# Copying node rows within memory during the sort, and making layer-1 node rows beside two attention hops

## What is computed

```python
# layer 0: attention over edges, then five propagation steps
s = leaky_relu(sum(tanh(x[src] @ W_h) * a_h) + sum(tanh(x[dst] @ W_t) * a_t) + s_rel[type])
A = 0.9 * segment_softmax(s, src)
Z = x for 4 heads
for _ in range(5):
    Z = segment_sum(A * Z[dst], src) + 0.1 * x
out = Z @ W_o
# x1 = x + out, then (out - mean) / sqrt(var + eps) over the 64 features   (a "layer-1 row")
# layer 1: four rounds of a graph convolution, layer 2: Chebyshev, layer 3: GIN with batch norm
```

## Time and profile before

| what | value |
|---|---|
| median of 3 runs | 10182.19 us (10180.14 to 10186.59) |
| profiled execution | 10185.65 us |
| its span | 10183.8 us |
| busy: PE, DVE, ACT, POOL | 57%, 66%, 30%, 70% |
| mean granted TensorE clock | 0.702 |
| HBM read, written | 852.84 MB, 795.02 MB |

### The profile page before, as it was taken

The page is one execution under the profiler, slowest core; times in us unless marked ns, Lnnn a source line. Parts: engine busy times, 40 slices in busy tenths (PEclk is TensorE's granted clock), DMA queues, the critical chain, the costliest instruction groups (busy, mean ns, idle before and its releaser), DMA issues. The chain is left out here.

```text
span 10183.8 us, 117523 instructions
## 1 busy us (share of the span) xinstructions
PE 5768.8 (57%) x28479; PEld 4109.1 (40%) x28479; DVE 6707.0 (66%) x13870; ACT 3105.4 (30%) x5997; POOL 7153.1 (70%) x7145
## 2 busy tenths in 40 slices
PE   3856999500000001886777786767774769833338
PEld 2453333100000001775666565555553658733336
DVE  8954333387878787996777786877775767622227
ACT  2542222163222222443434342222221432200006
POOL 2564777577777777777777676767776767677764
PEclk9978999755555555887877897777676775555559
DMA  0074333164545454437867676654444984311127
GB/s 14 7 244 125 73 72 74 36 212 156 167 145 166 147 166 135 128 121 187 222 214 227 208 259 203 229 166 142 136 135 132 332 271 131 106 46 47 45 63 278
DMA packets 1256873, 1519.22 MB, mean 149 GB/s; under 512 B 835537, under 2 KB 956719, under 8 KB 1256634
## 3 DMA queue, kind: packets, MB, share of 16 engines
q1 hardware_dynamic: 995656, 1253.98, 37.8%
q0 software_dynamic: 252192, 248.44, 11.0%
q10 hardware_dynamic: 8786, 14.21, 0.4%
HBM read 852.84 MB, written 795.02 MB: 162 GB/s over the span
## 5 line engine op out<-in xcount | busy, mean ns | idle before, releaser
L2764 POOL DMA_INDIRECT r_got<-state,comb_src x1176 | 1139.3, 969 | 367.6 <-issue 344.1
L336 POOL DMA_INDIRECT payload_or_bias_rows<-payload,place x784 | 779.1, 994 | 477.7 <-issue 252.2
L1949 PE MATMUL hop_ps_into<-hop_out,span_s 128*128 128x256 f32 x8 | 4.9, 715 | 1865.6 <-DVE hop_out L1759 1865.6
L1540 POOL DMA_INDIRECT hop_got<-edges_b,next_col x784 | 825.0, 1052 | 254.9 <-issue 237.5
L1540 POOL DMA_INDIRECT hop_got<-edges_a,next_col x784 | 782.6, 998 | 259.4 <-issue 238.5
L1949 PEld LDWEIGHTS hop_ps_into<-hop_out,span_s 128*128 128x128 f32 x8 | 2.0, 311 | 1866.2 <-DVE hop_out L1759 1866.2
L3043 PE MATMUL r_ps_v<-dense1g,r_gt 128*128 128x128 f32 x4312 | 752.8, 343 | 0.0
L3043 PEld LDWEIGHTS r_ps_v<-dense1g,r_gt 128*128 128x128 f32 x4312 | 681.2, 247 | 160.6 <-issue 160.6
L1838 ACT COPY hop_got<-hop_zeros 128x1792 f32<-128x1792 f32 x224 | 378.1, 1688 | 1091.3 <-DVE hop_ps_msg L1704 1082.0
L2924 DVE TENSOR_REDUCE r_stat<-r_sq 128x14 f32<-128x896 f32 x448 | 483.9, 1080 | 272.9 <-ACT r_sq L3097 271.5
L2869 DVE SCALAR_TENSOR_TENSOR r_acc<-r_acc,r_runs_now,r_got 128x64 f32<-128x64 f32 (+1 forms) x1564 | 447.9, 286 | 254.0 <-DMA r_got<-state,comb_src 197.9
(11 more groups left out here) (779 smaller groups left out, 17457.9 us busy)
## 6 DMA issues: line engine op xcount, KB each, us to landing
state<-r_y SPq DMA_DIRECT2D x252, 448.0 KB, 3.7
r_in<-state SPq DMA_DIRECT2D x252, 448.0 KB, 4.5
edges_a<-hop_out SPq DMA_DIRECT2D x112, 896.0 KB, 4.3
edges_b<-hop_out SPq DMA_DIRECT2D x112, 896.0 KB, 4.3
hop_side<-x_dst SPq DMA_DIRECT2D x280, 224.0 KB, 4.0
own<-plain_y SPq DMA_DIRECT2D x56, 952.0 KB
g_rows<-r_gx SPq DMA_DIRECT2D x112, 448.0 KB, 2.6
x_and_sums<-c_y SPq DMA_DIRECT2D x56, 896.0 KB
```

What stands on the lines that cost most here:

```text
L336: nc.gpsimd.indirect_dma_start(out=t.raw[:, n, :], out_offset=None, in_=t.pay[k], in_offset=bass.IndirectOffsetOnAxis(t.place[:, k, n:n + ...
L1540: pool.indirect_dma_start(out=got[:, u, c, :], out_offset=None, in_=table, in_offset=at, bounds_check=EP - 1, oob_is_err=False).then_inc(g ...
L2764: pool.indirect_dma_start(out=got[:, n, c - b * CT, :], out_offset=None, in_=table, in_offset=bass.IndirectOffsetOnAxis(idx[:, at + c:at + ...
```

## The change

- The sort's block: ScalarE, right after it stores the payload rows, issues 18 copies from `x` straight to `t.nodes1`, within memory: 8 for the second half of the wide rows (272 bytes a row, taken from `x` with the first numbers of the next row behind it), 2 for the last row of each partition, 8 for the first half (256 bytes a row). Nobody waits for them in this block. The clears go to SP, behind `store_keys`.
- `EARLY` is 250 and `UNDER_DEGREES` 272: 42 more payload gathers lie in the histogram, 22 (for 14) in the degrees' block, 120 (for 170) in the block behind it.
- `plain_rows` is gone. `store_marks` takes its place: 8 stores of 16 bytes for each node into the wide rows, four on SP and four on ScalarE; SP waits for them and for the copies.
- The target's part of a wide row is now gathered from its start, `[x, marks]`, 68 numbers and not 65.
- Hops 1 and 2 each make the layer-1 rows of half the nodes, 7 columns of 128 a turn, and SP stores them over the copied `x` in the first 64 numbers of the wide rows.

```diff
-EARLY = 208
-UNDER_DEGREES = 222
+EARLY = 250
+UNDER_DEGREES = 272
@@ sort_sources, ScalarE
-            act.wait_ge(blank_made, 1)
...
+            for n in range(X_PIECES):
+                lo_n, hi_n = n * J // X_PIECES, min((n + 1) * J // X_PIECES, J - 1)
+                with_next = bass.AP(x.tensor, x.offset + lo_n * D, [[J * D, P], [D, hi_n - lo_n], [1, ROW]])
+                act.dma_start(places[:, lo_n:hi_n, PLAIN:WIDE], with_next).then_inc(t.x_placed, 16)
...
+            for n in range(X_PIECES):
+                some = slice(n * J // X_PIECES, (n + 1) * J // X_PIECES)
+                act.dma_start(places[:, some, X1], given[:, some, :]).then_inc(t.x_placed, 16)
             act.wait_ge(pay_put, 16)
@@ store_marks (for plain_rows)
+        def pieces(eng, parity):
+            places = t.nodes1.rearrange("(p j) w -> p j w", p=P)
+            for n in range(parity, MARK_PIECES, 2):
+                some = slice(n * J // MARK_PIECES, (n + 1) * J // MARK_PIECES)
+                eng.dma_start(places[:, some, MARKS:MARKS + 4], t.marks[:, some, :]).then_inc(stored, 16)
@@ edge_pass of hops 1 and 2, SP: behind the side load of this turn, ahead of the result store of the last
+                        for i, u in ago(0):
+                            past(sp, xt_done, i, u, 2)
+                            sp.dma_start(xin[:, u % 2], w["x"]...[:, node_columns(i, u), :]).then_inc(xin_in[u], 16)
+                        for i, u in ago(3):
+                            sp.wait_ge(xy_ready[u], i + 1)
+                            sp.dma_start(t.nodes1...[:, node_columns(i, u), X1], xy[:, u]).then_inc(xy_kept[u], 16)
@@ VectorE: behind the linked sums of this turn
+                    for i, u in ago(2):
+                        dve.wait_ge(xroot_ready[u], i + 1)
+                        nc.vector.reciprocal(xstat[:, u % 2, 2, :], xstat[:, u % 2, 1, :]).then_inc(xinv_ready[u], 1)
+                    for i, u in ago(1):
+                        dve.wait_ge(xsq_ready[u], i + 1)
+                        nc.vector.tensor_reduce(xstat[:, u % 2, 0, :], xsq[:, u % 2], AX.X, ALU.add).then_inc(xsum_ready[u], 1)
@@ ScalarE: at the start of the turn
+                    for i, u in ago(2):
+                        act.wait_ge(xsum_ready[u], i + 1)
+                        nc.scalar.activation(xstat[:, u % 2, 1, :], xstat[:, u % 2, 0, :], ACT.Sqrt, scale=1.0 / D, bias=eps[:]).then_inc(xroot_ready[u], 1)
@@ ScalarE: behind the run flags and the scaled side rows of this turn
+                        act.wait_ge(xt_done[u], i + 1)
+                        nc.scalar.copy(gx[:, u % 2, 0:3 * P], ps_aside[:, 0:3 * P])
+                        nc.scalar.copy(gx[0:D, u % 2, 3 * P:], ps_aside[0:D, 3 * P:]).then_inc(gx_ready[u], 1)
+                    for i, u in ago(3):
+                        act.wait_ge(xinv_ready[u], i + 1)
+                        for c in range(CT):
+                            ins = nc.scalar.activation(xy[:, u, c, :], xy[:, u, c, :], ACT.Copy, scale=xstat[:, u % 2, 2, c:c + 1])
+                        ins.then_inc(xy_ready[u], 1)
@@ ScalarE: behind the zeroing of this turn
+                        act.wait_ge(xv_done[u], i + 1)
+                        nc.scalar.copy(xy[:, u]..., ps_into[:, 0:CT * D])
+                        nc.scalar.activation(xsq[:, u % 2]..., ps_into[:, 0:CT * D], ACT.Square).then_inc(xsq_ready[u], 1)
@@ TensorE, which had no work in the turns of these hops
+                        pe.wait_ge(xin_in[u], (i + 1) * 16)
+                        ... three transposes of 128x128 and one of 128x64 into ps_aside ... .then_inc(xt_done[u], 1)
+                        pe.wait_ge(gx_ready[u], i + 1)
+                        ... three products and one of 64x64 with t.dense0 into ps_into ... .then_inc(xv_done[u], 1)
@@ attention
+                  first_node=(0, J // 2, None)[k - 1])
```

More of the change, by code:

```diff
@@ L546, in _ @@
             store_keys(sp, t, 0, (y, z)[SORTED % 2][:], raw, kept, reloaded)
+            sp.wait_ge(blank_made, 1)
+            clears = 0
+            for tab in (t.edges_a, t.edges_b, t.cheb_rows):
+                sp.dma_start(tab[EP:EP + P, :], blank[:, 0:tab.shape[1]]).then_inc(cleared, 16)
+                clears += 1
+            for tab in (t.x3a[NP:NP + 512, :],):
+                rows = tab.rearrange("(p r) w -> p (r w)", p=P)
+                for a in range(0, rows.shape[1], blank.shape[1]):
+                    b = min(rows.shape[1], a + blank.shape[1])
+                    sp.dma_start(rows[:, a:b], blank[:, 0:b - a]).then_inc(cleared, 16)
+                    clears += 1
+            sp.wait_ge(cleared, 16 * clears)
             sp.wait_ge(reloaded, 48)
@@ L1400, in _, with edge_pass @@
                 c.link(nc.vector.scalar_tensor_tensor(t.att_e[:], e[:], 0.9, tot[:], ALU.mult, ALU.mult))
-def edge_pass(nc, t, name, kind, runs, span, fix, table=None, idx=None, put=None, target=None, after=None, w=None, aside=None):
+def edge_pass(nc, t, name, kind, runs, span, fix, table=None, idx=None, put=None, target=None, after=None, w=None, aside=None, first_node=None):
     heads = kind in ("heads", "heads_out")
@@ L1515, in chained, with node_columns @@
             return linked, (order(i, u) + 1) * CT
+        def node_columns(i, u):
+            return bass.ds(order(i, u) * CT + first_node, CT)
         def finished(i, u):
@@ L1629, in _ @@
                         sp.wait_ge(y1_kept[u], ROUNDS * 16)
+            if first_node is not None:
+                for u in range(RING):
+                    sp.wait_ge(xy_kept[u], ROUNDS * 16)
             if aside == "weights":
@@ L1847, in _ @@
                                              ACT.Relu).then_inc(msg_ready[u], 1)
+                if first_node is not None:
+                    for i, u in ago(0):
+                        act.wait_ge(xv_done[u], i + 1)
+                        wait(act, xy_kept[u], i * 16)
+                        nc.scalar.copy(xy[:, u].rearrange("p c d -> p (c d)"), ps_into[:, 0:CT * D])
+                        past(act, xsum_ready, i, u, 2)
+                        nc.scalar.activation(xsq[:, u % 2].rearrange("p c d -> p (c d)"), ps_into[:, 0:CT * D], ACT.Square).then_inc(xsq_ready[u], 1)
                 if rows_too:
@@ L1961, in attention @@
         edge_pass(nc, t, f"hop{k}", "heads", t.runs_s, t.span_s, t.fix_edge, table=a, idx=t.next_col, target=b,
-                  after=range(first, first + AFTER_HOP), w=w, aside=("weights", "targets", "degrees")[k - 1])
+                  after=range(first, first + AFTER_HOP), w=w, aside=("weights", "targets", "degrees")[k - 1],
+                  first_node=(0, J // 2, None)[k - 1])
     recycle(nc)
@@ L2033, in _ @@
         def _(sp):
-            @staged(sp, TURNS4, RING, KEEP)
-            def _(ago):
-                for i, u in ago(0):
-                    wait(sp, x_copied[u % 2], pair_order(i, u) - 1)
-                    sp.dma_start(in0[:, u], rows(x, i, u, D)).then_inc(in0_ok[u], 16)
-                for i, u in ago(KEEP):
-                    after(sp, y_ready, i, u)
-                    after(sp, x_copied, i, u)
-                    sp.dma_start(rows(t.nodes1, i, u, WIDE), y[:, u % 2]).then_inc(y_stored[u % 2], 16)
@@ L2069, in _ @@
[L2069 to L2086 removed]
+            pieces(sp, 0)
@@ L2111, in node_degrees @@
+            pieces(act, 1)
 def node_degrees(nc, t):
@@ L2139, in _ @@
             dve.wait_ge(loaded, 48)
+            nc.vector.memset(t.marks[:, :, 3], 0.0)
             c.link(nc.vector.tensor_scalar(t.plain[:], index[:], float(N), None, ALU.is_lt))
@@ L3795, in four_layers @@
         recycle(nc)
-        with nc.sbuf_tensor("marks", [P, J, 3], F32) as t.marks:
+        with nc.sbuf_tensor("marks", [P, J, 4], F32) as t.marks:
             node_degrees(nc, t)
-            plain_rows(nc, t, w["x"])
+            store_marks(nc, t)
         recycle(nc)
```

165 lines of the change are left out of this document (61 added, 104 removed).

## The result

| what | before | after |
|---|---|---|
| median | 10182.17 us (4 runs) | 10431.42 us (10425.17 to 10435.65, 4 runs) |
| ratio | | 1.0247, 95% interval 1.0232 to 1.0262 |
| profiled execution, its span | 10185.65, 10183.8 us | 10435.65, 10433.8 us |
| busy: PE, DVE, ACT, POOL | 57%, 66%, 30%, 70% | 57%, 63%, 32%, 69% |

The change costs 249 us (2.5%).

The account below looks back on a forecast made before the run. Limits differ by stage: VectorE in the histogram, DMA engines in the node-row block, GpSimd in hops 1 and 2, where SP's ring was to take over. Front -124 plus hops +152 gave +28: 10210 us, range 10105 to 10400.

Parts of the forecast that it names:

- Beside the sort: Sorted keys going to memory and back beside the copies: with queues sharing fairly, two transfers double their moving part, 3 us.
- the front's sum: Stages ahead of hop 1: 127 us saved by the marks' block, 3 us lost beside the sort, -124 us.
- the copies block the sort: Rival: ScalarE sits in the sort's block or SP's key store waits behind copies; histogram 75 to 205 us later; chance 0.20.
- Key chain: Sort's block: sorted keys stored and loaded back, a chain of two transfers beside the copies, 3 us more.
- Length of the copies: Copies within memory from 11 us: 12,544 pieces on each engine take 216 or 344 us, done by 227 to 357.
- the upper row: Cost of a copied piece taken from random gathered rows of 266 bytes, 27.6 ns on an engine: 344 us of copies.
- Marks: Block of mark stores: 6,272 16-byte pieces per engine take 68, 108 or 172 us; 108 taken, hidden under 150 us of gathers.
- Front without the hold: Histogram to the marks' block's successor: with gathers moved earlier, the next block starts at 707 instead of 834, -127 us.
- The hops: Hops 1 and 2 with layer-1 rows added: a turn of 10.5 us, costing 79 and 73 us.
- SP's ring: Hops 1 and 2: each input load waits for the previous one to pass TensorE and ScalarE, 10.5 us a turn.
- VectorE's ring: Hops 1 and 2: VectorE's reduce, ScalarE's root and side-row scaling, then VectorE's next add, 9.6 us a turn.
- Sum: Whole kernel: front -124 us and hops +152 us give +28, so 10210 us.

Follow-up runs that it names:

- one_transfer: Changed kernel, but ScalarE copies the second half in two small transfers and one of 100,224 pieces, SP the first half in one transfer; 10275.09 us, 1.0087 to before.
- split_copies: Changed kernel, but eight first-half copies stay on ScalarE in the sort and ten second-half copies go to SP in the histogram; 10227.20 us, 1.0046 to before.

## Why the prediction was wrong

Predicted 10210 us in 10105 to 10400; it was 10431. The failed step is the term "Beside the sort", 3 us in the front's sum. It asked whether short transfers get past the backlog and took for granted that the engine which issues the backlog gets away. It measured 196 us at the histogram's start. The case stood among the rivals as "the copies block the sort", with ScalarE sitting in the block, at 0.20, and gave 10285 to 10415. The range was meant to leave out its upper half, but its end at 10400 leaves out only the last 15 us of it. The rival's upper end, with 344 us of copies from 11 us on where ScalarE was held for 349, came 16 us short: the histogram's end moved by a little less than it had (199 us, and it had 205 on top of the 3), but the degrees' block and the hops took 15 us more than the sum and the stages behind hop 3 13 us more.

The other steps, one by one:

- *Key chain.* "each of the two transfers about doubles its moving part: 3 us". It was 18.5 us (178.04 against 159.57), seen as such in one_transfer. SP's key store was not blocked by ScalarE's queue, but its two transfers took 7 and 11 us longer while the DMA engines had the copies' pieces. The Trainium skill (DMA: Bandwidth & Descriptors, "Queues, rings and completion order") speaks of rounds between rings, and the keys did get past 200 us of backlog; by this trace a chain of two short transfers came 18.5 us late where I had 3. That the rounds are what took this time is not shown.
- *Length of the copies.* Bounds of 216 and 344 us: ScalarE's hand-overs took 349 us here and 332 in two other executions, and the pieces moved until about 378, so the upper row was nearest, though its reason (a random row) was not. The second half takes nearly twice as long as the first (29 and 15.7 us a transfer), by the ends of its pieces. The Trainium skill's read-modify-write under 512 bytes (DMA: Bandwidth & Descriptors, "Specifications") is not what separates them: both halves are under 512 bytes.
- *Marks.* 6,272 pieces an engine at 17.2 ns, 108 us: they took about 135 us (756 to 891), 21.5 ns. Hidden, as the 120 gathers took until 908.9; 18 us were left.
- *Front without the hold.* -127: -121 measured. The degrees' block took 34.4 us (721.6 to 756.0) with its gathers, where the forecast had 29 and the kernel before took 23. With the copies split the whole front to hop 1 gave -131.
- *The hops.* 10.5 us a turn: 10.50 and 10.60. +79 and +73: +81.1 and +80.5. SP's ring was forecast as 0.25+6.7+1.2+2.33 us; the timeline has 0.25 us to SP, 6.35 from the store of `xy` to TensorE, 1.15 to ScalarE's copies, and 2.3 from there to the end of the scalings, 10.06 in this turn; the eleven turns from 2603 us on go from 10.1 to 11.1, 10.48 in the mean. VectorE's ring, forecast at 9.6, is 9.48 once it binds. Both rings are shown by removing them one after the other.
- *Sum.* -124+152 = +28 forecast, +77+162 = +239 found; of the 211 between, 196 are the histogram's later end (+198.6 for +3), 5 the degrees' block behind it and 10 the hops.

## What to carry to other kernels

A transfer of very many small pieces is not free for the engine that issues it: here the next issue on that queue lasted until the large transfer ahead had been moved (106 us behind 50,176 pieces). Put such transfers on an engine with nothing else in the block, as its last issues, and let them be done before a short chain through memory begins (here it came 18.5 us late beside them). When work is added to a stage with slack in busy time, walk round every loop of waits through in-order queues: here one wait put a turn back and one root put behind two other instructions took 1.5 us off each of 112 turns. Neither that wait nor the split copies alone brought the change below the kernel before; together they did.

## What the runs showed of the hardware that I had not expected

- The hand-over rule above: 100,224 pieces in 0.68 us, but the next one, large or small, held for 106 to 109 us behind one of 50,000 pieces of 272 bytes, 63 us behind one of 50,176 pieces of 256 bytes, and 24 to 31 us behind one of 12,500 pieces of 272 bytes.
- Pieces within memory by their ends: 20.0 ns each on an engine (256 bytes, both ends on multiples of 32 bytes, 205 GB/s over the core), 21.2 ns (288 bytes, both on, 217 GB/s), 37 ns (272 bytes, one end off), 61 ns (256 bytes, both off, 67 GB/s), 29 ns (16 bytes, one off). The ends are those in the wide rows, which the pieces are written to. Half of the pieces at 20 and 21 ns begin at an odd multiple of 32 bytes, so more than 32 isn't asked for; that 16 would not do is what those at 37 and 61 ns show.
- Copies with a DMA share of 0.91 over the histogram's stretch of the earlier trace rows did not slow VectorE, 304.04 of 320 us busy, and hardly GpSimd, which did 229 gathers there and 234 in the changed kernel's histogram, at a DMA share of 0.14. The row is of split_copies:

```profile
166.00:486.00 320.00, 285.81 (x1573) 147.69 (x1574) 304.04 (x1355) 192.88 (x331) 236.97 (x229) 0.98 0.91 92
```
